# Value taps of a linear-attention block summed in two accumulators that TensorE adds as it transposes them

## What is computed

```python
f = chan_ln(x, norm_g)
q = dwconv3x3(conv1x1(f, q_w), q_dw)
k = dwconv3x3(conv1x1(f, k_w), k_dw)
v = dwconv3x3(conv1x1(f, v_w), v_dw)          # 3x3, depthwise, zero padding
q, k, v = map(to_heads, (q, k, v))            # (B*8, 256, 16)
q = softmax(q, axis=-1) * scale
k = softmax(k, axis=-2)
ctx = einsum('bnd,bne->bde', k, v)
out = silu(einsum('bnd,bde->bne', q, ctx))    # back to channels
x = chan_ln(conv1x1(out, out_w), out_norm_g) + x
out = x + conv1x1(chan_ln(gelu(conv1x1(chan_ln(x)))))
```

## Time and profile before

| | us |
|---|---|
| median of 3 runs | 83.91 (83.77 to 83.94) |
| the profiled execution, its own time | 83.64 |
| its span, first to last instruction | 81.8 |
| PE busy | 71.5 |
| DVE busy | 57.2 |
| ACT busy | 48.7 |
| POOL busy | 30.5 |
| granted TensorE clock | 1.000 of full |

### The profile page before, as it was taken

The page is one execution under the profiler, slowest core; times in us unless marked ns, Lnnn a source line. Parts: engine busy times, 40 slices in busy tenths (PEclk is TensorE's granted clock), DMA queues, the critical chain, the costliest instruction groups (busy, mean ns, idle before and its releaser), DMA issues.

```text
span 81.8 us, 1629 instructions
## 1 busy us (share of the span) xinstructions
PE 71.5 (87%) x563; PEld 53.7 (66%) x563; DVE 57.2 (70%) x210; ACT 48.7 (60%) x133; POOL 30.5 (37%) x62
## 2 busy tenths in 40 slices
PE   4978999999999997939898999999998579779960
PEld 1325799847888775737456656998997277646830
DVE  1357887897678649776688243699999838898540
ACT  4300487368843608395968398997998634627530
POOL 7913450005953364000000030488878712155400
PEclk9999999999999999999999999999999999999999
DMA  1999700000000000000000000000000000000003
GB/s 17 204 331 404 288 0 0 0 0 8 0 4 0 4 0 0 0 0 8 0 0 0 8 0 0 0 0 0 8 0 4 0 0 0 4 0 0 0 3 126
DMA packets 1304, 2.91 MB, mean 36 GB/s; under 512 B 144, under 2 KB 784, under 8 KB 1296
## 3 DMA queue, kind: packets, MB, share of 16 engines
q1 hardware_dynamic: 1152, 2.68, 9.8%
q10 hardware_dynamic: 144, 0.13, 0.5%
HBM read 2.55 MB, written 0.26 MB: 34 GB/s over the span
## 4 chain that ended last, share of the span: by engine, by line
PE 63%; DVE 17%; POOL 7%; ACT 4%; DMA 3%; issue 2%; POOLq 0%
PE bank L1213 9%; DVE nmx L748 6%; PE bank L1112 5%; PE bank L1151 4%; DMA x<-in_x 3%; POOL vacc L269 3%; POOL rs L221 3%; PE bank L1290 3%; PE bank L1138 2%; PE bank L1055 2%; PE bank L1001 2%; PE bank L973 2%; PE bank L944 2%; PE bank L1038 2%; PE bank L1124 2%
## 5 line engine op out<-in xcount | busy, mean ns | idle before, releaser
L221 POOL TENSOR_TENSOR rs<-ve,mhalf 128x2 f32<-128x2 f32 x8 | 5.6, 696 | 23.2 <-DVE ve L533 23.1
L269 POOL TENSOR_TENSOR vacc<-vacc,vprod 128x240 f32<-128x240 f32 (+1 forms) x16 | 10.8, 675 | 5.5 <-ACT vprod L412 3.8
L376 ACT ACTIVATE pT<-bank 128x512 f32<-128x512 f32 x16 | 8.5, 602 | 1.7 <-PE bank L1138 1.3
L1213 PE MATMUL bank<-convw,fsh 128*128 128x128 f32 x72 | 9.2, 275 | 0.0
L1213 PEld LDWEIGHTS bank<-convw,fsh 128*128 128x128 f32 x72 | 8.7, 193 | 0.1
L748 DVE TENSOR_REDUCE nmx<-bank 128x2 f32<-128x512 f32 x10 | 6.4, 687 | 3.2 <-PE bank L1112 3.2
L240 POOL TENSOR_TENSOR convw<-wgc,tapw 128x128 f32<-128x128 f32 x9 | 3.8, 453 | 8.0 <-DVE wgc L699 8.0
L412 ACT ACTIVATE vprod<-bank,wc 128x256 f32<-128x256 f32 x16 | 6.6, 492 | 0.0
L792 DVE SCALAR_TENSOR_TENSOR kacc<-bank,wc,kacc 128x240 f32<-128x240 f32 (+1 forms) x16 | 6.3, 447 | 0.0
L910 PE MATMUL bank<-warm 128*128 128x512 bf16 x13 | 4.8, 517 | 1.2 <-DVE warm L535 1.2
L1112 PE MATMUL bank<-km,qm 32*128 32x256 f32 x64 | 4.6, 400 | 0.0
(11 more groups left out here) (215 smaller groups left out, 186.9 us busy)
## 6 DMA issues: line engine op xcount, KB each, us to landing
wc<-in_pack_c SPq DMA_DIRECT2D x1, 649.0 KB, 6.7
wb<-in_pack_b SPq DMA_DIRECT2D x1, 612.0 KB, 5.6
tapw<-in_taps SPq DMA_DIRECT2D x1, 576.0 KB, 7.6
wa<-in_pack_a SPq DMA_DIRECT2D x1, 320.0 KB, 4.5
out<-y SPq DMA_DIRECT2D x2, 128.0 KB, 1.7
x<-in_x ACTq DMA_DIRECT2D x1, 128.0 KB, 2.8
x<-in_x SPq DMA_DIRECT2D x1, 128.0 KB, 2.7
wa<-in_pack_a SPq DMA_DIRECT2D x1, 72.5 KB, 2.6
```

Source lines behind the costliest of these rows:

```text
L221: nc.gpsimd.tensor_tensor(dst, src, mhalf[:, 0:width], ALU.pow).then_inc(done, 1)
L269: nc.gpsimd.tensor_add(vacc[b][:, oy, ox], vacc[b][:, oy, ox], vprod[n - 1][b][:, iy, ix]).then_inc(s[f"vsum_d{b}"], 1)
L376: nc.scalar.activation(pT2[u % PT2_RING][:, :, :], tiles(bank[SCORE_T_BANKS[u % HG]]), ACT.Exp).then_inc(s["e2_d"], 1)
L1213: product = nc.tensor.matmul(LA[b][:, j * C:(j + 1) * C], fsh[dx][b][:, row:row + H // NT, :].rearrange("p h w -> p (h w)"), convw[:, 3 * ...
```

## The change

A second accumulator, vodd, is added per image, cleared by POOL ahead of the block. Product n = 1 goes straight into vodd at its shifted place, with no add; the even products are added to vacc and the odd ones to vodd, so that a sum waits for the sum two before it. There are seven adds per image instead of eight, and seven vprod tiles. PE's transposes become matmuls with the identity as moving operand, two per half that accumulate in PSUM: vacc with start, vodd with stop.

```diff
-        vacc = per_batch("vacc", [128, H, W])
-        vprod = [per_batch(f"vprod_{n}", [128, H, W]) for n in range(TAPS - 1)]
+        vacc, vodd = per_batch("vacc", [128, H, W]), per_batch("vodd", [128, H, W])
+        vprod = [per_batch(f"vprod_{n}", [128, H, W]) for n in range(TAPS - 2)]
@@ POOL
             for b in range(NB):
                 nc.gpsimd.memset(kacc[b][:, 1, :, :], 0.0).then_inc(s["cleared"], 1)
+                nc.gpsimd.memset(vodd[b][:, :, :], 0.0).then_inc(s["cleared"], 1)
@@ POOL, v_sums
                         (oy, ox), (iy, ix) = shifted(*CENTRE_FIRST[n])
+                        acc = (vacc, vodd)[n % 2][b][:, oy, ox]
                         pool.wait_ge(s[f"vprod_d{b}"], n + 1)
-                        if n > 1:
-                            pool.wait_ge(s[f"vsum_d{b}"], n - 1)
-                        nc.gpsimd.tensor_add(vacc[b][:, oy, ox], vacc[b][:, oy, ox], vprod[n - 1][b][:, iy, ix]).then_inc(s[f"vsum_d{b}"], 1)
+                        if n > 3:
+                            pool.wait_ge(s[f"vsum_d{b}"], n - 3)
+                        nc.gpsimd.tensor_add(acc, acc, vprod[n - 2][b][:, iy, ix]).then_inc(s[f"vsum_d{b}"], 1)
@@ POOL's order: v_sums(1, 4) and v_sums(1, TAPS) begin at 2
@@ ACT, v_products
-                        dst = vprod[n - 1][b][:, :, :] if n else vacc[b][:, :, :]
-                        nc.scalar.activation(dst, LC[b][:, 0:N].rearrange("p (h w) -> p h w", h=H), ACT.Copy,
-                                             scale=tap("vdw", *CENTRE_FIRST[n])).then_inc(s[f"vprod_d{b}"], 1)
+                        src = LC[b][:, 0:N].rearrange("p (h w) -> p h w", h=H)
+                        dst = vprod[n - 2][b][:, :, :] if n > 1 else vacc[b][:, :, :]
+                        if n == 1:
+                            (oy, ox), (iy, ix) = shifted(*CENTRE_FIRST[n])
+                            dst, src = vodd[b][:, oy, ox], src[:, iy, ix]
+                        nc.scalar.activation(dst, src, ACT.Copy, scale=tap("vdw", *CENTRE_FIRST[n])).then_inc(s[f"vprod_d{b}"], 1)
@@ PE, v_transposes
-                pe.wait_ge(s[f"vsum_d{b}"], TAPS - 1)
-                for t in range(NT):
-                    last = nc.tensor.transpose(LB[b][:, t * C:(t + 1) * C],
-                                               vacc[b][:, t * (H // NT):(t + 1) * (H // NT), :].rearrange("p h w -> p (h w)"), ident)
+                pe.wait_ge(s[f"vsum_d{b}"], TAPS - 2)
+                for t in range(NT):
+                    rows = slice(t * (H // NT), (t + 1) * (H // NT))
+                    for acc in (vacc, vodd):
+                        last = nc.tensor.matmul(LB[b][:, t * C:(t + 1) * C], acc[b][:, rows, :].rearrange("p h w -> p (h w)"), ident,
+                                                start=(acc is vacc), stop=(acc is vodd))
                 last.then_inc(s["v3_p"], 1)
```

More of the change, by code:

```diff
@@ L265, in stage @@
                         (oy, ox), (iy, ix) = shifted(*CENTRE_FIRST[n])
+                        acc = (vacc, vodd)[n % 2][b][:, oy, ox]
                         pool.wait_ge(s[f"vprod_d{b}"], n + 1)
-                        if n > 1:
-                            pool.wait_ge(s[f"vsum_d{b}"], n - 1)
-                        nc.gpsimd.tensor_add(vacc[b][:, oy, ox], vacc[b][:, oy, ox], vprod[n - 1][b][:, iy, ix]).then_inc(s[f"vsum_d{b}"], 1)
-                return stage
-            for stage, b in ((xb2_sum, 0), (key_steps, 0), (xb2_sum, 1), (key_steps, 1), (root3, 0), (v_sums(1, 4), 0), (root3, 1),
-                             (v_sums(4, TAPS), 0), (v_sums(1, TAPS), 1), (root4, 0), (root4, 1), (root5, 0), (root5, 1), (root6, 0),
+                        if n > 3:
+                            pool.wait_ge(s[f"vsum_d{b}"], n - 3)
+                        nc.gpsimd.tensor_add(acc, acc, vprod[n - 2][b][:, iy, ix]).then_inc(s[f"vsum_d{b}"], 1)
+                return stage
+            for stage, b in ((xb2_sum, 0), (key_steps, 0), (xb2_sum, 1), (key_steps, 1), (root3, 0), (v_sums(2, 4), 0), (root3, 1),
+                             (v_sums(4, TAPS), 0), (v_sums(2, TAPS), 1), (root4, 0), (root4, 1), (root5, 0), (root5, 1), (root6, 0),
                              (root6, 1)):
```

## The result

| | before | after |
|---|---|---|
| median, us | 83.94 (83.77 to 85.11, 5 runs) | 83.34 (83.13 to 83.47, 5 runs) |
| ratio | 1 | 0.9941, 95% interval 0.9924 to 0.9958 |
| the profiled execution, us (span) | 83.64 (81.8) | 83.13 (81.3) |

A forecast was written before the change was run, and what follows sets the result against it. PE was taken as the bound, its wait for POOL's last sum of image 1 giving 1.31 us slack. Earlier v_transposes -0.26, upstream -0.31 and held k_max +0.10 sum to -0.47: 83.91 becomes 83.4, range 83.1 to 84.0.

The forecast's parts named there:

- Term B: Upstream, ve3 of image 1 no longer held by a POOL add, so PE's later queue comes earlier: -0.31 us, bounds 0 and -0.31.
- Term C: DVE's k_max of each image can be held by a POOL add: +0.1 us taken, bounds 0 and 0.5.
- 0.67 us of PE per image: v_transposes become 8 instructions instead of 2, six more at 0.112 us: 0.67 us more per image.
- The sums leave the path: POOL's sums of image 1 end by 63.7 to 64.8, before PE could start v_transposes at 65.01.
- Rival 4: POOL still pays 0.14 per add, yet is not waited for: also 83.4 us, no chance of its own.
- Image 0's passes shift DVE by 0.44: Image 0's extra 0.67 on PE delays the convolution, so q_max of image 1 and DVE's queue behind it shift 0.44.
- What is late next: With the sums gone, o3_product of image 0 is next late, waiting for its DVE mask queued behind q_max.
- Rival 3: Slower by held DVE in image 1's stretch, upstream gain failing too: +0.24 to +0.74, 84.2 us taken, chance 0.14.
- the break-even: v_transposes of image 1 must start before 65.27 to gain; without the upstream gain DVE may slip 0.26 beyond 0.44.
- Rival 1: No upstream gain, ve3 still held; only the -0.26 from v_transposes of image 1 remains: 83.65 us, chance 0.20.

The follow-up runs named there:

- e1: Kernel before with only PE's four accumulating matmuls in v_transposes, the second accumulator staying zero: 84.33 us, ratio 1.0055.
- e9: Changed kernel with each POOL sum waiting for the one right before it: 83.26 us, ratio 0.9942.
- e4: Kernel before with one ve3 instruction of image 1 as tensor_reduce, that norm's epsilon left out: 84.68, 84.88, 85.09 and 83.38 us, too little for a ratio.
- e3: Changed kernel with the centre key tap last and written to PSUM, so k_max reads one SBUF input: 83.09 us, ratio 0.9911.
- e8: Changed kernel with POOL joining the accumulators and single PE transposes in image 0 only: 83.31 us, ratio 0.9942.
- e7: The change in image 1 only; image 0 keeps eight serial sums and single transposes: 83.46 us, ratio 0.9973.
- e2: Changed kernel, but POOL adds vodd to vacc as an eighth sum and PE transposes once, both images: 82.75 us, ratio 0.9856.
- e5: Changed kernel with both e2's POOL join and e3's PSUM operand for k_max: 82.41 us, ratio 0.9842.
- e6: The change in image 0 only; image 1 keeps eight serial sums and single transposes: 83.11 us, ratio 0.9933.
- e10: The same kernel as e4, measured in more rounds: ratio 1.000 (0.9968 to 1.0032) against the kernel before.
- e11: e4's kernel with ten bf16 matmuls on zeros on PE before its wait for image 1's sums: 83.47 us, ratio 0.996 to the kernel before.
- e12: Kernel before with the same ten matmuls as e11 in PE's wait for image 1's sums: 83.55 us, ratio 0.998.

## Why the prediction was right, point by point

The total (-0.47) met the measured -0.50, and the sign was right; the sums of image 1 left PE's path, as foreseen. v_transposes of image 1 start at 64.79; the terms put them at 65.01 - 0.31 + 0.10 = 64.80. That closeness is in part luck, in terms B and C.

- **0.67 us of PE per image**: right. The eight of image 1 fill 0.89 us, 64.79 to the start of ff_mean at 65.68, 0.111 each; e1 shows 0.72 for six.
- **The sums leave the path**: right, and e9 shows that even serial ones would have. Rival 4 gave the same time, as said.
- **Term B, -0.31**: the convolution's next matmul at 55.80 instead of 56.13, 0.33, of which 0.07 was there before the block (v_1x1 of image 0 at 50.40 against 50.47): 0.26. Right in mechanism, 0.05 too large. (The old start of the second f_transpose was put at 55.97; the row gives 55.71 + 0.58 - 0.28 = 56.01. Nothing hangs on it.) e4 adds a condition I had not stated, that POOL itself must be free.
- **Image 0's passes shift DVE by 0.44**: right as a size, wrong as the delay that binds. With k_max not held (e3) q_max waits for the convolution and starts at 62.95, as the term says (62.84 + 0.44 less B and the 0.07). With k_max held it starts at 63.07 with the passes and without them (e8).
- **Term C, +0.10**: the one term mis-sized as a hold, and right by luck as a price. k_max of image 1 was held 0.50 (0.93 less 0.42), the upper bound. I took 62.44, where k_max met the last 0.19 us of an add, as evidence that a hold is cheap; it only showed how much of the add was left. Its release is 0.14 before the add's recorded end there (62.44 + 0.47 - 0.42 = 62.49 against 62.63), 0.15 for ve3 (54.31 against 54.46), and 0.13 in the changed kernel (62.21 + 0.93 - 0.42 = 62.72 against 62.85). Image 0's k_max was held 0.20; e3 frees both, and the price of the two together is the 0.10 to 0.12 of its rows.
- **Why the sum still held**: the two delays lie side by side, not one behind the other. q_max waits for the later of the convolution (62.95 in e3) and k_max (63.07). The hold of 0.50 costs only what it reaches beyond the passes, 0.12. I had added 0.44 and 0.10 in a row; that 0.10 for a cheap hold is so near the 0.12 that a dear one leaves is luck. The prediction did say that q_max would wait for PE for longer, but the sum has no term for it.
- **What is late next**: I named o3_product's mask; right, it starts at 63.86 behind q_max, and PE waits for ek_transposes (0.47) on the way.
- **Rival 3**, slower by a held DVE with B gone too, had the right place and the full hold, but added it to the 0.44. e7 has k_max held 0.93 and ve3 held 0.56, and is still faster than the kernel before (0.9973), not 0.24 slower: its v_transposes of image 1 start at 65.04 (65.15 on the scale of the kernel before), ahead of the 65.27 that was the break-even. It lacks image 0's passes, which e8 shows to be hidden beside a held k_max; the exact case of rival 3 was not run. Rival 1 needs B to fail as well, and e7's 83.46 is the nearest run to its 83.65.

## What to carry to other kernels

When two accumulators are added by TensorE, count the passes: an fp32 add on PE took 0.67 us of PE per image where a GpSimd join in idle time cost nothing, and moving it gave about as much again as the change (e2). Of the two images only image 1's passes were on the path (e8). Two delays that end within 0.12 us of each other must both go before more than that arrives: q_max came 0.12 sooner in e3, not at all in e8, and 0.45 in e5. Look at every DVE instruction with two SBUF inputs beside a stream of GpSimd adds: the price is nearly what is left of the running add, and closing the gaps between the adds can raise it: k_max of image 1 took 0.43 to 0.73 with serial sums beside it (e9, the kernel before, e6) and 0.92 or 0.93 with overlapping ones (the changed kernel, e2, e7, e8).

## What was not expected of the hardware

**The lock by the form of the instruction.** The Trainium skill ("SBUF — State Buffer", "Who interferes with whom") lets a tensor_scalar in a 2-port mode and a DVE instruction with two SBUF inputs contend with GpSimd, and a tensor_reduce, or an instruction with one SBUF input outside those modes, not. The traces agree each time: ve3 as tensor_scalar 0.55, as tensor_reduce 0.15; k_max with two SBUF inputs 0.93, with one 0.42. The page has the lock held for the whole instruction; here DVE went on 0.13 to 0.15 us before the recorded end of the add. It works the other way too: an add that began 0.04 behind k_max took 0.91, and in the changed kernel one behind k_max of image 0 took 0.87 and one behind q_norm's multiply 0.82, where its others take 0.60 to 0.70.

**The clock falls behind an idle PE.** PE's granted clock was 1.00 throughout the profile of the kernel before, but not in e4's and e10's, which have the same wait of 1.16 us for the sums. e4, stretches of 2 us, and its PE:

```profile
62.00:64.00 2.00, 1.49 (x10) 0.96 (x9) 1.73 (x6) 1.62 (x5) 1.57 (x4) 1.00 0.00 0
64.00:66.00 2.00, 0.84 (x5) 0.57 (x4) 1.18 (x4) 0.41 (x2) 1.24 (x2) 0.90 0.00 0
66.00:68.00 2.00, 2.00 (x10) 1.72 (x9) 0.49 (x2) 0.77 (x2) 0.00 (x0) 0.50 0.00 0
68.00:70.00 2.00, 2.00 (x13) 1.95 (x13) 1.23 (x7) 0.45 (x2) 0.00 (x0) 0.75 0.00 0
```
```profile
65.44 0.59 PE L1231 MATMUL bank<-wa,vacc 128*128 128x128 f32 x2 [1.16 <-POOL vacc L269]
65.82 1.06 PE L962 MATMUL bank<-w1g,wc 128*128 128x256 f32 x2
...
67.10 1.06 PE L1244 MATMUL bank<-v,ekT 128*128 128x128 f32 x4
```

(Columns of the first: stretch, length, busy PE, PEld, DVE, ACT, POOL, granted clock, DMA share, GB/s.) The granted clock falls from its full level, 2.4 GHz, to 1.2 GHz just behind PE's 1.16 us of idle time (it is at 1.00 up to 65.4); PE had been busy for 1.49 of the 2 us from 62 and for 0.84 of those from 64. ctx_product's four instructions take 1.06 instead of 0.69. Such an execution costs about 1.2 us and has a mean clock of 0.977 to 0.980. It happened in 21 of the 77 executions of the kernel before that ran beside the experiments, in 8 of 16 of e4 and e10, and in none of 83 of the other kernels. Among these are 24 of e11 and e12, which are e4's kernel and the kernel before with PE kept at work in the wait. Why it falls in one execution of a kernel and not in the next, and in more of e4's and e10's than of the kernel before, stays open. So removing PE's wait removes a risk as well, which the ratios hardly count.
